# Fifteen identity products instead of thirty-two at the head of an adaptive-layernorm block

## What is computed

```
mod = silu(c) @ wmod                      # c: 2 x 512, wmod: 512 x 3072
sa, ca, ga, sb, cb, gb = mod              # shift, scale and gate of both layers
h = layernorm(x) * (1 + ca) + sa          # x: 2 x 1024 x 512
x = x + ga * attn(h)                      # conv (3 taps, 512 -> 3*128), 16 heads of 64, blocks of 128, causal
h = layernorm(x) * (1 + cb) + sb
x = x + gb * ffn(h)                       # dense 512 -> 512 plus 16 low-rank experts, top 2
```

## Time and profile before

| | us |
|---|---|
| median of 3 runs | 461.55 |
| lowest and highest run | 459.86 and 462.46 |
| profiled execution, device time | 460.72 |
| its span | 458.9 |
| TensorE busy in it | 432.5 (94%) |
| VectorE busy in it | 348.9 (76%) |

### The profile page before, as it was taken

The page is one execution under the profiler, slowest core; times in us unless marked ns, Lnnn a source line. Parts: engine busy times, 40 slices in busy tenths (PEclk is TensorE's granted clock), DMA queues, the critical chain, the costliest instruction groups (busy, mean ns, idle before and its releaser), DMA issues.

```text
span 458.9 us, 11354 instructions
## 1 busy us (share of the span) xinstructions
PE 432.5 (94%) x4270; PEld 284.8 (62%) x4270; DVE 348.9 (76%) x683; ACT 300.7 (66%) x976; POOL 268.3 (58%) x313
## 2 busy tenths in 40 slices
PE   8899989999999989989999999988999999788996
PEld 8466558678787657654678666646676665344442
DVE  4697798988999978868678775668887988654851
ACT  1463778998897969866667866656778776721220
POOL 5021842451457986747667737463648778876681
PEclk9999989999999999999999999989999999999999
DMA  8995376752756497487572696518554472861542
GB/s 314 372 384 212 51 181 165 197 101 47 139 125 152 54 202 149 129 177 149 120 156 48 104 179 111 117 56 148 110 116 93 90 157 55 144 134 38 127 111 70
DMA packets 140678, 64.06 MB, mean 140 GB/s; under 512 B 130480, under 2 KB 130736, under 8 KB 140240
## 3 DMA queue, kind: packets, MB, share of 16 engines
q1 hardware_dynamic: 140480, 63.32, 60.0%
q10 hardware_dynamic: 144, 0.02, 0.0%
HBM read 26.63 MB, written 4.19 MB: 67 GB/s over the span
## 4 chain that ended last, share of the span: by engine, by line
PE 60%; DVE 15%; DMA 8%; POOL 7%; ACT 4%; SPq 3%; issue 2%; POOLq 0%; ACTq 0%
PE C L1175 15%; PE F L1047 15%; PE C L1047 11%; DMA gT<-g 5%; PE W L1238 4%; DVE cw L890 3%; PE W L1047 3%; PE S L1221 3%; PE S L1047 3%; PE F L1064 2%; DMA xb<-in_x_dram 2%; DVE g L1030 2%; ACT prob L724 2%; POOL prob L599 2%; PE S L1213 1%
## 5 line engine op out<-in xcount | busy, mean ns | idle before, releaser
L1175 PE MATMUL C<-hT,cw 128*128 128x256 f16 x864 | 109.2, 276 | 2.7 <-DVE cv L908 2.0
L599 POOL TENSOR_TENSOR prob<-prob,rinv 128x1024 f32<-128x1024 f32 x32 | 60.7, 1896 | 65.1 <-DVE rinv L942 65.0
L1175 PEld LDWEIGHTS C<-hT,cw 128*128 128x128 f16 x864 | 83.4, 99 | 21.5 <-issue 2.6
L724 ACT ACTIVATE prob<-S,nms 128x128 f32<-128x128 f32 x256 | 89.9, 377 | 4.1 <-DVE p L937 3.2
L1047 PE MATMUL F<-btw,gT 128*128 128x512 f16 x336 | 76.6, 385 | 6.0 <-DMA gT<-g 6.0
L695 ACT ACTIVATE qk<-C,bqk 128x256 f16<-128x256 f32 x128 | 52.7, 486 | 23.4 <-PE C L1047 22.9
L917 DVE SCALAR_TENSOR_TENSOR qk<-C,bqk,qk 128x256 f16<-128x256 f32 x128 | 54.5, 475 | 9.1 <-ACT qk L695 8.6
L1047 PEld LDWEIGHTS F<-btw,gT 128*128 128x128 f16 x336 | 32.6, 99 | 46.1 <-DMA gT<-g 7.4
L724 ACT ACTIVATION_READ_ACCUMULATOR prob<-S,nms 128x1 f32 x256 | 55.5, 217 | 0.0
L1047 PE MATMUL C<-cv,pw 128*128 128x256 f16 x384 | 51.6, 277 | 2.1 <-DVE xb L958 1.9
L937 DVE SCALAR_TENSOR_TENSOR p<-prob,p 128x1024 f16<-128x1024 f32 x32 | 45.7, 1427 | 3.6 <-ACT p L733 3.5
(11 more groups left out here) (198 smaller groups left out, 753.3 us busy)
## 6 DMA issues: line engine op xcount, KB each, us to landing
xa<-in_x_dram SPq DMA_DIRECT2D x10, 512.0 KB, 4.9
xb<-in_x_dram SPq DMA_DIRECT2D x6, 512.0 KB, 5.2
wmb<-in_wmod_dram SPq DMA_DIRECT2D x1, 3072.0 KB, 17.7
out_dram<-xb SPq DMA_DIRECT2D x12, 256.0 KB, 2.0
cw_raw<-in_cw_dram SPq DMA_DIRECT2D x3, 768.0 KB, 10.6
raw<-in_cw_dram SPq DMA_DIRECT2D x3, 768.0 KB, 5.3
wma<-in_wmod_dram SPq DMA_DIRECT2D x4, 512.0 KB, 6.8
bt_raw<-in_btw_dram SPq DMA_DIRECT2D x2, 1024.0 KB, 5.7
```

The source lines that it names most:

```text
L599: nc.gpsimd.tensor_tensor(prob[:], prob[:], rinv[:, i % 2].unsqueeze(2).broadcast_to([P, 8, P]), ALU.mult).then_inc(p_normal, 1)
L724: ins = nc.scalar.activation(prob[:, h], S[i % len(S)][h // 4][:, (h % 4) * P:(h % 4 + 1) * P], ACT.Exp, bias=nms[:, i % 2, h:h + 1], scal ...
L1175: ins = nc.tensor.matmul(bank_c[:, 0:CH], cw[:, i, a, c, tap, :], hT[:, j % 2, b, c, OWN - 1 + tap:OWN - 1 + tap + CH], start=step == 0, s ...
```

## The change

The number of identity products at TensorE's head goes from 32 to 15. Nothing else is touched: the order of all other instructions, on every engine, is the same.

```diff
     QUAD = 32
-    N_CONST, N_IDENT, N_WARM = 12, 3, 32
+    N_CONST, N_IDENT, N_WARM = 12, 3, 15
     C_COND = 3 + 3 * NC + 1
```

## The result

The changed kernel took 465.65 us (median of 4 runs, 462.50 to 465.86), the kernel before in the same sessions 460.71 us (458.56 to 462.46): a ratio of 1.009, 95% interval 1.0048 to 1.0132. The forecast was 457.7 us, with 455.7 to 460.3 us as its range. Taken together it is somewhere between 0.3% faster and 1.3% slower, and the 0.8% of gain is not there in either. Why three of the first four runs took 465.6 to 465.9 us, and only one of the twelve later ones as much (466.1 us), stays open. The ratios leave out runs that are over 1.5% above the fastest of the same kernel, so where there are such runs the tables give the median of all and, behind it, that of the others.

A forecast was written before the change was run, and what follows sets the result against it. TensorE's order of work up to `row_ab` was taken as the bound at the start; 34 removed passes x 0.1118 us = 3.80 us, nothing charged behind, gave 461.55 - 3.80 = 457.75 us, range 455.7 to 460.3 us.

The forecast's parts named there:

- The bound at the start: From 1.68 to 16.4 us the order on TensorE is the bound, up to VectorE's copy into `row_ab`.
- the passes' price: At TensorE's head, the 34 removed passes all ran at full clock, 0.1118 us each, worth 3.80 us.
- the landings: First loads land before TensorE needs them; slice 1 of `wma`, at 8.6 us, is tight and charged 0 to 0.1 us.
- the case of an early rise: At the head, TensorE's clock rises 1.9 us earlier, the changed kernel waits for slice 1, and the gain is 2.9 us.
- From there on every start is set by another instruction of the kernel, which moves along: Behind `row_ab` the 3.8 us shift passes to the end; shared loads cost 0 to 0.2 us, taken as 0.
- the sum: Over the whole kernel, 3.80 us gained less nothing: 461.55 - 3.80 = 457.75 us on the median.
- Rival 1: At TensorE's idle gaps, one half-clock stretch more (459.45 us, chance 0.12) or fewer (456.05 us, 0.08), at most 1.7 us each.
- Rival 2: At the start, a wait stands at a fixed time, likely a load; gain 0 to 2 us, middle 460.5 us, chance 0.06.
- Rival 3: At the start, 15 products leave TensorE's clock low: +1.0 us, or up to 465.5 us; chance 0.04.
- The range: For the whole kernel, 455.7 to 460.3 us: from one half-clock stretch fewer to an early rise with one more.

The follow-up runs named there:

- again15: The changed kernel with 15 identity products run once more, nothing edited: 461.86 us (median of 12), ratio 1.0007 to the kernel before.
- short_i128: Against the kernel before, 4 float32 and 56 bf16 products at the head: about 15 products' length, the 128 instructions of 32; 457.36 us, ratio 0.9942.
- long_i60: Against the kernel before, 6 wide and 9 128x128 products at the head: 32 products' length, the 60 instructions of 15; 466.56 us, ratio 1.0071.
- again32: The kernel before with 32 identity products run once more, nothing edited: 460.59 us (median of 12), ratio 0.9996.

## Why the prediction was wrong, by its own steps

- **The bound at the start, the passes' price, the landings:** right. 3.80 us were forecast and 3.79 us measured. (The 0.22 us a pass at 1.2 GHz is a little too much: 26 passes, two of them not in the trace, begin in the 5.57 us to the first row at the higher level, 0.214 us each. It enters the case of an early rise alone.) The first product with `wma` began at 7.47 us and not 7.79 us, since the clock rose at 5.7 us in this execution, but then waited for slice 1 until 8.65 us, as the case of an early rise said. In again15 and short_i128 the gain at `row_ab` is 3.6 us.
- **"From there on every start is set by another instruction of the kernel, which moves along":** this is the step that failed, and with it the sum, which charged nothing behind the start. The loads and semaphores do move along. TensorE's instruction packets do not: they follow the instruction count, and I had costed the removed instructions by their time alone. The 68 instructions moved 34 packets against 76 transposes. With the instruction count held the shorter head has a ratio of 0.9942, a gain of 2.7 us (short_i128), and with the length held the lower count has 1.0071, a loss of 3.3 us (long_i60). The product of the two is 1.0013, and the 15-product kernel, which has both, came out at 1.0007 (0.997 to 1.004, again15). Its first four runs, at 1.009 (1.005 to 1.013), lie above that, and what made them so much slower is not shown.
- **Rival 1** (other half-clock stretches, 1.7 us each) named something real and missed its cause. A stretch of it costs 1.69 us at the F products, as priced. But it was called a matter of chance; the longer `gT` flight makes the gap 2.6 to 2.7 us in all four traces with 60 instructions at the head, and the clock fell behind three of them, while it fell behind none of the eight gaps of 1.5 to 2.0 us. The collision behind it, 3.05 us, stood in no case of mine.
- **Rival 2** had the outcome (gain given back, by something on the DMA side) with the wrong carrier. It named landings of the first loads; those came on time.
- **Rival 3** (no clock) did not happen: the clock was up at 5.7 us. The transposes of the first chunk ran at 0.11 us from start to start in the changed kernel too, at the full granted clock. The Trainium skill's sentence that transposes do not engage the full clock ("TensorE: Matmul & The Clock Gate", "Part 4: PE-mode transpose") had no effect here that a row shows. The half-clock stretch at 16 us is not put down to them: again32, with all 32 products, had one at 19 us.
- **The range** left out rivals 2 and 3, one in ten together. It was made of the start's uncertainties and of one stretch more or less, and these are under 2 us each; the 29 runs of the kernel before beside again15, which came later, spread from 458.4 to 465.5 us.

## What to carry to other kernels

An instruction that is removed or added has a length and a count. In a kernel whose engines hang on DMA transposes, look at the packets of the instruction queue as one looks at any other load, and vary the count at constant length (wider or narrower products that nobody reads) before a small edit is called good or bad: here heads of 5.8 to 6.4 us gave 457.3, 457.4, 460.0 and 461.8 us with 16, 128, 96 and 60 instructions (medians of the runs that the ratios use). Follow a gain through the kernel by matching instructions: in the first trace of the change it shows the one place where 5.5 us went, and in again15 that the loss is spread over several.

## What the runs showed of the hardware

- TensorE's instructions arrive in packets of 16 KB, 34 here, each in DMA service for 0.9 to 1.7 us. A DMA transpose in whose flight (or up to 0.3 us ahead of it) one began landed 1.03 us later than at its best (median of 241), one without 0.02 us (of 519). The same `gT` was in flight for 5.3 us without one, 5.7 to 6.1 us with one 0.8 to 1.0 us after its issue, and 6.4 to 6.5 us with one 3.0 to 3.2 us after it. Why a packet should delay a transpose was not tested.
- VectorE's split of a 128x384 float32 tile took 0.61 us alone and 1.62 us beside a float32 addition of GpSimd (128x512); GpSimd's addition took 1.57 us there against 1.27 us.
- The same kernel's executions differed in where the clock rose first (5.3 us in again32, 7.1 us in the trace before, 7.4 us in again15) and in which idle gaps were followed by a half-clock stretch.
